# An expert's 186 slots as 126 + 60 over the partitions, and two takeovers of rows moved ahead on VectorE

## The reference, cut to what matters

```
h = tokens(x)                            # patches @ W + b, class token, positions: [32, 37, 256]
h = h + attention(layernorm(h))          # products of factors of rank 64, running sums over the 37 tokens
h = h + experts(layernorm(h))

experts(x), for the 1184 tokens:
  logits = x @ w_router + b_router       # 8 experts
  gates = softmax(logits);  topv, topi = top 2 of gates
  pos  = how many choices of that expert came earlier, in the order of the tokens
  keep = pos < 185                       # an expert takes 185 choices at most
  buf[e, pos] = x[token] where keep
  out[e] = gelu(buf[e] @ w1[e] + b1[e]) @ w2[e] + b2[e]     # 256 -> 1024 -> 256
  y[token] = sum over its kept choices of gate * out[e, pos], divided by the sum of these gates
```

## Time and profile before

| | |
|---|---|
| median of three runs | 163.95 us |
| the profiled execution's own time | 163.92 us |
| its span (first to last instruction) | 162.1 us |
| mean granted clock of TensorE | 0.995 |
| TensorE (PE) busy | 153.8 us, 95% |
| VectorE (DVE) busy | 107.3 us, 66% |
| ScalarE (ACT) busy | 83.0 us, 51% |
| GpSimd (POOL) busy | 51.8 us, 32% |

### The profile page before, as it was taken

How to read it: one execution, slowest core, us unless ns; L and a number is a source line. 1 busy time by engine, 2 the same in 40 slices (tenths; PEclk the granted TensorE clock), 3 DMA queues, 4 the chain that set the end, 5 groups by cost and what they waited for, 6 DMA issues and landing times.

```text
span 162.1 us, 3124 instructions
## 1 busy us (share of the span) xinstructions
PE 153.8 (95%) x1055; PEld 145.5 (90%) x1055; DVE 107.3 (66%) x344; ACT 83.0 (51%) x208; POOL 51.8 (32%) x52
## 2 busy tenths in 40 slices
PE   7999999999999899989999999999999999999950
PEld 7669999988799799889989999899999999999950
DVE  0067683598467897975598956859578596694610
ACT  4306453482246979434326665567573774746200
POOL 3005340007140000002707528267083480703351
PEclk9999999999999999999999999999999999999998
DMA  5999950088005444300299996886978868710422
GB/s 164 426 424 411 396 179 0 2 293 276 0 0 135 121 133 131 86 4 0 73 291 295 265 269 146 293 250 190 279 162 317 259 186 262 189 25 0 47 24 23
DMA packets 17263, 28.47 MB, mean 176 GB/s; under 512 B 1289, under 2 KB 13875, under 8 KB 17125
## 3 DMA queue, kind: packets, MB, share of 16 engines
q1 hardware_dynamic: 14789, 25.48, 46.5%
q0 software_dynamic: 2464, 2.86, 10.3%
HBM read 24.20 MB, written 4.14 MB: 175 GB/s over the span
## 4 chain that ended last, share of the span: by engine, by line
PE 82%; DVE 6%; DMA 4%; issue 2%; POOLq 1%; POOL 1%; ACT 0%; DVEq 0%
PE ps L1234 21%; PE ps L1256 10%; PE ps L1153 7%; PE ps L1083 7%; PE ps L1138 7%; DMA patch_t<-w 4%; PE ps L1258 4%; PE ps L1168 3%; PE ps L1242 3%; PE ps L1063 2%; PE ps L1195 2%; PE ps L1095 2%; PE ps L1266 2%; PE ps L1173 2%; PE ps L1181 1%
## 5 line engine op out<-in xcount | busy, mean ns | idle before, releaser
L491 POOL DMA_INDIRECT out_rows<-out_s,dst_row x16 | 23.8, 1485 | 39.3 <-ACT out_s L653 32.9
L629 ACT ACTIVATE first_t<-ps,b_cur 128x186 f32<-128x186 f32 x64 | 23.1, 412 | 25.3 <-PE ps L1234 25.2
L1256 PE MATMUL ps<-hid_hl,split 128*128 128x372 f32 x96 | 29.0, 369 | 0.0
L476 POOL DMA_INDIRECT rows_in<-xrows,src_row x14 | 15.8, 1129 | 32.4 <-DVE src_row L916 28.4
L1258 PE MATMUL ps<-hid_hl,split 128*128 128x186 f32 x96 | 23.9, 249 | 0.0
L1234 PE MATMUL ps<-first_t,w_even 128*128 128x186 f32 x128 | 21.8, 322 | 0.7 <-DVE first_t L938 0.7
L1234 PE MATMUL ps<-first_t,patch_t 128*128 128x186 f32 x128 | 21.7, 322 | 0.3 <-DVE first_t L938 0.3
L951 DVE CAST hid_hl<-first_t 128x372 fp32r<-128x372 f32 x28 | 10.8, 387 | 15.6 <-ACT first_t L629 15.5
L1234 PEld LDWEIGHTS ps<-first_t,w_even 128*128 128x128 f32 x128 | 20.1, 190 | 1.0 <-issue 1.0
L1234 PEld LDWEIGHTS ps<-first_t,patch_t 128*128 128x128 f32 x128 | 20.1, 190 | 0.6 <-issue 0.6
L514 ACT ACTIVATE split<-patch_t 128x512 fp32r<-128x512 f32 (+1 forms) x28 | 13.9, 556 | 9.0 <-DMA patch_t<-patches 4.9
(11 more groups left out here) (175 smaller groups left out, 280.8 us busy)
## 6 DMA issues: line engine op xcount, KB each, us to landing
w_even<-w SPq DMA_DIRECT2D x8, 1024.0 KB, 5.6
patch_t<-w SPq DMA_DIRECT2D x8, 1024.0 KB, 5.7
patch_t<-patches SPq DMA_DIRECT2D x2, 972.0 KB, 10.9
att<-attn SPq DMA_DIRECT2D x1, 1280.0 KB, 8.2
first_t<-first SPq DMA_DIRECT2D x1, 870.0 KB, 5.8
out_rows<-h SPq DMA_DIRECT2D x3, 288.0 KB
xrows<-xn SPq DMA_DIRECT2D x3, 288.0 KB, 2.4
first_t<-first SPq DMA_DIRECT2D x1, 580.0 KB, 4.1
```

The costliest lines, as they stand in the source:

```text
L476: pool.indirect_dma_start(out=rows_in[q][0:SIZES[s], s, :], out_offset=None, in_=xrows[:, :], in_offset=bass.IndirectOffsetOnAxis(ap=src_r ...
L491: pool.indirect_dma_start(out=out[:, :], out_offset=bass.IndirectOffsetOnAxis(ap=dst_row[0:SIZES[s], c:c + 1], axis=0), in_=out_s[q][0:SIZ ...
L629: ins = act.activation(hid[:, f, :], bank(pair)[:, (f % 2) * SL:(f % 2 + 1) * SL], ACT.Gelu, bias=b1_cur[q][:, f:f + 1])
L1256: pe.matmul(dst[:, 0:2 * SL], w2_h[q][:, f, cols], hid_hl[:, f].rearrange("p a s -> p (a s)"), start=f == 0, stop=False)
```

## The change

`ST` becomes 126, so that `SIZES` is 126 and 60. VectorE makes all marks of slots in one instruction, behind the takeover of the picked rows. The takeover of expert 1's rows stands ahead of the reading of the weights.

```diff
-ST = 96
+ST = 126
 SIZES = [min(ST, SL - s * ST) for s in range(SLOT_TILES)]
@@
-            find_slots(0, 3)
             take_in(0, 0, first=True)
-            step(find_slots(3, NT))
+            step(find_slots(0, NT))
@@
             read_ids()
             weigh_tokens()
+            take_in(1, 1)
             read_weights()
-            take_in(1, 1)
             for e in range(2):
                 dve.tensor_copy(coef_cur[e][:, :], coef[:, e * SLOT_TILES:(e + 1) * SLOT_TILES]).then_inc(coef_ready, 1)
             read_out(0, 0)
```

## The result

The changed kernel takes 167.82 us (median of four runs, 167.32 to 168.15). The kernel before took 163.64 us in the runs beside it. The ratio is 1.0274, 95% interval 1.0238 to 1.031: 4.2 us lost, far outside the forecast range. The profiled execution of after took 168.14 us, with a span of 166.0 us at a mean granted clock of 0.994, against 163.92 and 162.1 at 0.995. So the clock is not the cause, and the two profiles differ by as much as the medians. One run of the kernel before beside experiments 5 to 7 took 314.61 us, and the ratios leave it out.

The account below looks back on a forecast made before the run. TensorE was taken to bound the kernel, with two short waits for VectorE and the tail. Terms -0.21 + 0 + 0.5 - 0.12 + 0 + 0 - 0.3 = -0.13 gave 163.8 us, range 162.9 to 164.7.

Parts of the forecast that it names:

- Step 5: Loop over experts: `turn_in` keeps its 186 moving columns and its time; 0 taken, upper bound 0.4 us lost over seven experts.
- Step 1: First takeover ahead of the marks: expert 0's first product comes 0.21 us earlier, bounds 0 and 0.3.
- Rival D: Expert 0's takeover and output: ScalarE's half starts later, output is waited for, both moves gain nothing; 164.1 us, chance 0.1.
- Step 2: All marks in one VectorE instruction of 3.04 us, hidden before the lookup's loads; cost 0, bounds 0 and 0.3 us.
- Rival C: Id marks end after TensorE's arrival at the lookup, up to 0.3 us of stall; 164.0 to 164.1 us, chance 0.12.
- Step 3: Two lookups with 126 stationary columns: 11 ns more for each of 44 products, 0.5 us lost, bounds 0 and 0.6.
- Step 4: Second takeover before the weights: TensorE's idle shrinks, expert 0's output comes later; net gain 0.12 us, bounds 0 and 0.23.
- Step 6: Last expert's two tiles: longer first and shorter second tile cancel; 0 taken, bounds -0.2 and +0.2 us.
- Step 7: Tail: last scatter of 60 rows takes 0.59 us instead of 0.89, GpSimd's instruction unchanged; gain 0.3 us, bounds 0 and 0.3.
- Rival A: Tail: GpSimd's scatter instruction also shrinks by a third, 0.5 us more gained; 163.3 us, chance 0.25.
- Rival B: Lookups and last expert's first tile: exposed wide stationary loads, lookups lose 1.1 us, not 0.5; slower, 164.4 us, chance 0.13.

Follow-up runs that it names:

- experiments 5 to 7: Kernel after with tiles of 121 and 65 (165.12 us), 122 and 64 (201.48 us); kernel before with added product of 60 (166.15), 66 (164.75) or 64 rows (166.83).
- experiment 10: Kernel before with marks behind first takeover, tiles 126 and 60, second tile's transposes padded to 66 rows, VectorE taking over both halves: 164.23 us, ratio 1.0049.
- experiment 8: Kernel before with only the takeover of expert 1's rows moved ahead of the reading of the weights: 163.65 us, ratio 1.0037.
- experiment 6: Kernel after with tiles of 122 and 64 slots instead of 126 and 60: 201.48 us against 163.27 of before, ratio 1.2334.

## Why the prediction was wrong, step by step

- **Step 5 failed, and with it the forecast.** It held that "moving columns of `turn_in` stay 186", and bounded the rest by the width of a transpose at 0.06 us an expert. The pace depends on more than moving columns: the stationary operand of the second transpose has 60 rows, and each change across 64 rows costs 0.14 to 0.17 us. It was 0.56 us in each turn of the loop. No row of before has a product of 64 rows or fewer (the smallest have 74), so no bound read from them could hold it; it had to be seen that 60 is a kind of operand that the trace does not show, and its bound left wide. That gathers have several us to land held in after, but the same step has no word on the weights, whose transfers land 1.3 us later (6.9 us instead of 5.6 in the median); that shows once the drains are gone (experiment 10).
- **Step 1: the mechanism was wrong, 0 instead of -0.21.** ScalarE's half was named as late next, but 0.16 us were taken for its release, from VectorE's copy. It takes 0.37 us before (68.99 to 69.36) and 0.36 after (69.08 to 69.44). So it was due at 69.36 in before whatever VectorE did; the trace named VectorE, which had ended nearer to the product. Rival D had this outcome for step 1, but not this reason.
- **Step 2 held.** 3.03 us for the marks (forecast 3.04), id marks done at 72.70, TensorE's load for the lookup at 73.15, no wait. Rival C falls.
- **Step 3 held.** 22 products take 1.23 us, 55.9 ns each, 11.8 ns more than before (11 assumed): 0.52 us lost in two lookups. The rule of the Trainium skill that the prediction quotes from "TensorE: Matmul & The Clock Gate", "LDWEIGHTS (loading the stationary operand)", would have given an estimate of 25 ns, twice that.
- **Step 4: right in the small, a side effect missed.** TensorE's idle 0.29 us went and `turn_out(0)` came 0.09 us later behind pair 0, as forecast. "Stand after 84 us" dismissed the work that the move pushes back by 0.4 us: with it, GpSimd's first scatter grows by 0.6 us, and the move is 0.37% slower by itself (experiment 8; that the one makes the other is not shown).
- **Step 6 held.** The first and second tile of the last expert take 117 ns a product.
- **Step 7 held in the sum.** The packets of the last scatter take 0.65 us (forecast 0.59; before they fill 18 slices of the earlier trace rows and not 17, 0.95 us, and two thirds of that are 0.63), GpSimd's instruction 1.43 instead of 1.47. From that instruction's start to the span's end pass 4.5 us instead of 4.9. Rival A falls. The filling up to a multiple of 16 rows gave the right number by luck: it is the largest divisor that counts (experiment 6), and for 60 and 90 rows both rules give the same packets.
- **Rival B** ended on the right side, slower, by a mechanism that did not happen: a product of the lookups lost 11.8 ns and not 25.
- **Two slips in the rivals' sums** decide nothing: rival B with step 5's bound is 164.4 + 0.4 = 164.8 us, not 164.7, and rival C's terms reach 163.8 + 0.2 + 0.3 = 164.3 us, not 164.1.
- **The sum of after**: first `turn_in` +0.43, six turns +3.4, lookups +0.52, step 4 -0.2, tail -0.35 give 3.8 us, against 3.9 between the spans, with no term for the late scatter.

## What to carry to other kernels

Before a tile is resized, list for each product that touches it on which side of 64 rows its stationary operand lies, and count the changes along TensorE's order; keep all above, pad a few rows of zeros, or group the small ones. Look at the row count of an indirect DMA for its largest divisor up to 16 before anything else: with 96 and 90 rows the scatters landed in 3.5 us in the median, with 126 and 60 in 4.1 to 4.7, and 122 cost the kernel 38 us. A loss in one stage can hide another one behind it, here most likely the later weights behind the drains, so add the terms up again when the first is taken out. And where two engines each hand over a half, the one named by the trace is the one that ended nearest; compare each one's usual time from end to release before crediting a gain to either.
